# A hybrid block on one core: the reciprocal of two softmax sums made by GpSimd as a power, not by VectorE

## The reference, cut to what matters

```python
def _gated_bottleneck(x2d, conv_w, conv_b, gamma, beta, lin_w, lin_b):
    xc = einsum('ngf,gf->ng', x2d.reshape(n, g, 4), conv_w) + conv_b
    xn = (xc - mean) * rsqrt(var + eps) * gamma + beta     # over all rows
    return gelu(xn) @ lin_w.T + lin_b                      # 256 logits a row

score_out = softmax(_gated_bottleneck(x, so_...))          # 256 scores a row
s_v, s_i = top_k(score_out, 32)
out_branch = zeros.at[s_i].add(take(x @ weight, s_i) * s_v)
score_in = softmax(_gated_bottleneck(x, si_...))
s_v, s_i = top_k(score_in, 32)
in_branch = zeros.at[s_i].add(take(x, s_i) * s_v) @ weight
return out_branch + in_branch + bias
```

## Time and profile before

| what | value |
| --- | --- |
| runs | 1357.16, 1364.52 and 1355.29 us, median 1357.16 us |
| the profiled execution | 1359.22 us, of which the span of the trace is 1357.5 us |
| mean granted clock of TensorE | 0.974 of full speed |
| busy share of the span | PE 90%, DVE 85%, ACT 78%, POOL 70% |
| sparse layer 1 (tile 0 to tile 31 on GpSimd) | 271.8 to 488.8 us |
| sparse layer 2 | 1170.2 us to the end |

### The profile page before, as it was taken

One profiled execution on the slowest core, in us unless ns is written; L12 is line 12 of the kernel. 1 busy time (PEld: TensorE's weight loads), 2 busy tenths in 40 slices (PEclk: granted clock), 3 DMA queues, 4 the chain that ended last, 5 costly groups with the idle time before them and its releaser, 6 DMA issues.

```text
span 1357.5 us, 30767 instructions
## 1 busy us (share of the span) xinstructions
PE 1222.2 (90%) x10252; PEld 751.2 (55%) x10252; DVE 1147.6 (85%) x3124; ACT 1052.3 (78%) x2347; POOL 954.4 (70%) x1098
## 2 busy tenths in 40 slices
PE   5999999688888889999999999999999999677776
PEld 2555554345445546666666666666666666344443
DVE  7999996797999988888777788877878854899998
ACT  3323424786999889999999989999999985877776
POOL 4367553486787777777776777777777773488887
PEclk9999999996999999999999999999999999898988
DMA  6200000100002000010000000000000000000000
GB/s 153 61 1 1 0 0 1 42 1 1 24 28 77 30 20 24 24 25 25 25 25 2 2 2 2 2 2 3 2 2 2 2 2 1 1 31 17 32 17 31
DMA packets 35529, 25.32 MB, mean 19 GB/s; under 512 B 16358, under 2 KB 32044, under 8 KB 35372
## 3 DMA queue, kind: packets, MB, share of 16 engines
q1 hardware_dynamic: 35372, 23.36, 6.1%
HBM read 14.89 MB, written 8.39 MB: 17 GB/s over the span
## 4 chain that ended last, share of the span: by engine, by line
PE 45%; ACT 12%; issue 11%; DVE 9%; POOL 4%; DVEq 0%; DMA 0%; ACTq 0%; POOLq 0%; SPq 0%
PE banks L2123 7%; PE banks L2125 7%; PE banks L2111 6%; PE banks L2064 4%; PE banks L2140 4%; PE banks L2141 4%; DVE arena L1595 4%; PE banks L2142 4%; ACT arena L1218 3%; DVE arena L1590 3%; ACT arena L1230 2%; PE banks L2040 2%; ACT arena L1066 2%; PE banks L2186 1%; PE banks L1987 1%
## 5 line engine op out<-in xcount | busy, mean ns | idle before, releaser
L877 POOL TENSOR_TENSOR arena<-arena 128x512 f16<-128x512 f32 x383 | 437.5, 1161 | 145.1 <-ACT arena L1230 141.3
L1218 ACT ACTIVATE arena<-banks 128x512 f32<-128x512 f32 x512 | 302.6, 599 | 41.8 <-PE banks L2125 37.4
L1674 DVE TENSOR_REDUCE arena<-banks 128x1 f32<-128x512 f32 x512 | 326.3, 680 | 4.8 <-PE banks L2111 2.6
L1230 ACT ACTIVATE arena<-arena 128x512 f16<-128x512 f32 x512 | 315.6, 631 | 0.0
L2140 PE MATMUL banks<-arena 128*128 128x65 f16 x2016 | 211.4, 193 | 1.0
L2141 PE MATMUL banks<-arena 128*128 128x64 f16 x2016 | 211.6, 195 | 0.0
L2142 PE MATMUL banks<-arena 128*128 128x65 f16 x2016 | 210.6, 193 | 0.0
L1700 DVE TENSOR_TENSOR arena<-arena 128x512 f16<-128x512 f32 x129 | 107.5, 834 | 121.4 <-ACT arena L1230 121.2
L1590 DVE MAX8 arena<-arena 128x8 f32<-128x256 f32 x512 | 190.0, 412 | 23.8 <-issue 13.7
L1595 DVE MATCH_REPLACE8 arena<-arena 128x256 f32<-128x256 f32 x512 | 205.7, 409 | 0.9 <-issue 0.4
L2140 PEld LDWEIGHTS banks<-arena 128*128 128x128 f16 x2016 | 187.9, 96 | 31.7 <-issue 9.9
(11 more groups left out here) (241 smaller groups left out, 2591.7 us busy)
## 6 DMA issues: line engine op xcount, KB each, us to landing
arena<-q_store SPq DMA_DIRECT2D x48, 128.0 KB, 2.7
x<-in_L_attn_a_x SPq DMA_DIRECT2D x8, 512.0 KB, 3.9
q_store<-arena SPq DMA_DIRECT2D x32, 128.0 KB, 1.8
out<-x SPq DMA_DIRECT2D x7, 512.0 KB, 2.9
arena<-arena SPq DMA_DIRECT2D x64, 1.0 KB, 1.9
arena<-in_L_attn_a_W_in SPq DMA_DIRECT2D x1, 768.0 KB, 5.8
arena<-in_L_attn_a_W_mid SPq DMA_DIRECT2D x1, 512.0 KB, 7.4
arena<-in_L_attn_a_w_w SPq DMA_DIRECT2D x2, 256.0 KB, 7.7
```

The lines of the kernel that those rows point to most:

```text
L877: nc.gpsimd.tensor_tensor(pr_lo[c][:, kt, :], pr[:, kt, :], pr_hi[c][:, kt, :], ALU.subtract).then_inc(a_lP, 1)
L1218: nc.scalar.activation(pr[:, kt, :], ps[6 + kt % 2][:, :], ACT.Exp, scale=SM_SCALE).then_inc(a_P, 1)
L1230: nc.scalar.activation(pr_hi[c][:, kt, :], pr[:, kt, :], ACT.Copy).then_inc(a_hi, 1)
L1674: nc.vector.tensor_reduce(mx_half[c][:, i // 2, i % 2:i % 2 + 1], ps[bank][:, :], X, ALU.max).then_inc(a_mx, 1)
```

## The change

`over_sums` moves from VectorE to GpSimd. There it is the first thing of `tail`, `tail_shared` and (after the row plus bias) `tail_last`, and it makes `sm` to the power of `minus_one`, with a `tensor_tensor` of 128 x 2. VectorE's waits for `ffn_gs` and `ffn_fs` two tiles back go with it, since GpSimd's `tail` has waited for both already. VectorE gets one new wait for `f_ri`, in the last tile of layer 2.

```diff
+            def over_sums(T, p):
+                pool.wait_ge(f_e, T * 2 + 2)
+                nc.gpsimd.tensor_tensor(rinv[p], sm[p], minus_one[:, 0:2], ALU.pow).then_inc(f_ri, 1)
+
             def tail(f, t, p):
                 T = t + f * NT
-                pool.wait_ge(f_e, T * 2 + 2)
+                over_sums(T, p)
                 pool.wait_ge(f_er, T * 2 + 1 + CREDIT["f_er"])
...
             def tail_shared(t, p):
                 T = t
-                pool.wait_ge(f_e, T * 2 + 2)
+                over_sums(T, p)
                 pool.wait_ge(f_er, T * 2 + 2 + CREDIT["f_er"])
...
                 nc.gpsimd.tensor_tensor(xb[p].unsqueeze(1), x[:, t:t + 1, :], fbias[:, :].unsqueeze(1),
                                         ALU.add).then_inc(f_xb, 1)
-                pool.wait_ge(f_e, T * 2 + 2)
+                over_sums(T, p)
                 pool.wait_ge(f_er, T * 2 + 2 + CREDIT["f_er"])
...
-            def over_sums(f, t, p):
-                T = t + f * NT
-                if not (isinstance(T, int) and T < 2):
-                    dve.wait_ge(f_gs, T - 1 + CREDIT["f_gs"])
-                    dve.wait_ge(f_fs, T - 1 + CREDIT["f_fs"])
-                dve.wait_ge(f_e, T * 2 + 2)
-                nc.vector.reciprocal(rinv[p], sm[p]).then_inc(f_ri, 1)
...
                 for t in range(NT):
                     topk_first(f, t, t % 2)
-                    if t:
-                        over_sums(f, t - 1, (t - 1) % 2)
                     if f == 0:
                         head_maxima(t - 2)
                     topk_rest(f, t, t % 2)
                     if f == 0:
                         head(t)
-                over_sums(f, NT - 1, 1)
...
                 dve.wait_ge(f_gps, T + 1)
                 dve.wait_ge(f_obx, T + 1)
+                dve.wait_ge(f_ri, T + 1)
```

## The result

The kernel after takes 1376.80 us (median of 4 runs, 1374.24 to 1381.35) against 1357.01 (4 runs): a ratio of 1.0152 with an interval of 1.0127 to 1.0176. It is slower, by 1.5%. The base is the three runs shown above and a fourth of 1356.87. The profiled execution took 1374.24 us, its span is 1372.5.

What follows compares the result with a forecast made beforehand. VectorE was taken to set layer 2's pace, with GpSimd 0.40 us a tile under it. Layer 1 +4.1 and layer 2 +11.0 sum to +15.1 us: 1374.3 profiled, 1372 as median against 1357.16; range 1362 to 1383.

Steps and rivals of the forecast that it cites:

- The bound changes engine in layer 2: Layer 2: GpSimd's pace becomes 6.10 us a tile, over VectorE's 5.76, so GpSimd sets the pace; head 30 +9.4 us.
- The power's price: GpSimd's tile heads: one 128 x 2 power takes 0.70 us and costs 0.65 a tile.
- GpSimd's "own pace" of 5.45 us: Layer 2, tile 2: GpSimd waits for no other engine, 5.45 us a tile, leaving 0.40 us of room under VectorE.
- Low clock: Layer 2: waits for TensorE's in-product at low clock, formerly absorbed by GpSimd's room, now count: +1.9 us.
- The rival of many more falls: Layer 2: TensorE, left idler, falls to its low clock far more often; 1379 to 1384 us, chance 12%.
- The last two tiles: End of layer 2: +9.4 us at head 30 becomes +9.1 at the end, as L799 no longer waits for ScalarE.
- Layer 1: Layer 1: +1.9 us by tile 6, +0.2 at tile 9, +1.95 in tiles 11, 15 and 19; together +4.1.
- the first rival: Layer 1, tiles 6 to 9: the slow-clock stretch goes away, head 9 at 329.1, total +7.8 us, 1365; chance 25%.
- The base: Kernel before: profiled execution 1359.22 us, median of the runs 2.06 lower at 1357.16.

Runs made afterwards that it cites:

- e4: Kernel after with the power replaced by a multiplication by -1 of the same shape, reciprocal left out: 1354.72 us beside 1354.40 for the kernel before.
- e11: Kernel after without GpSimd's bias addition `xb` in all but each layer's last tile, power still at the head: 1377.15 us beside 1355.49 for the kernel before.
- e13: Kernel after without `xb` in all but each layer's last tile, and the power moved behind `sx`: 1354.75 us beside 1354.30 for the kernel before.
- e7: Kernel before plus an unread 128 x 4 power on GpSimd at each tile's head: 1397.20 us beside 1355.04 for the kernel before.
- e8: Kernel before plus three TensorE products of zeros ahead of the wait for `sx`, in layer 2 and layer 1's first twelve tiles: 1358.31 us beside 1355.04.
- e9: Kernel after plus three TensorE products of zeros ahead of the wait for `sx`, in layer 2 and layer 1's first twelve tiles: 1371.87 us.
- e6: Kernel before plus an unread 128 x 2 power on GpSimd at each tile's head: 1377.28 us beside 1354.40 for the kernel before.
- e1: Kernel after with the power on GpSimd in layer 2 alone, layer 1 keeping VectorE's reciprocal: 1372.24 us beside 1354.40 for the kernel before.
- e2: Kernel after with the power on GpSimd in layer 1 alone, layer 2 keeping VectorE's reciprocal: 1367.34 us beside 1354.40 for the kernel before.

## Why the prediction came out, step by step

- **The bound changes engine in layer 2: right.** Head 1 to head 30: forecast 29 x 6.10 = 176.9 and 1.9 of low-clock waits, together 178.8; measured 179.34.
- **The power's price: right.** Forecast 0.70 long and 0.65 a tile, measured 0.702 and 0.67 (5.44 to 6.11). The Trainium skill, "GPSIMD Engine Reference", section "Performance versus the Vector engine", gives elementwise operations a price by their elements and has none for a power. Priced so, it would have been like any operation of two columns; the plain one in e4 (0.195 us, nothing lost) shows what would then have happened.
- **GpSimd's "own pace" of 5.45 us: right number, wrong owner.** I read in the earlier trace rows that it waits for no other engine. It does: `ob` starts when `fs` has arrived, and no wait is shown because `xb` covers all but 0.1 us of it. The 5.45 us are the round. e11 and e13 tell the two apart. The sum came out because the power was put into the round, and because work and round are near each other: in the kernel after, L793 to L797 are 0.84 us where neighbours without a wait are 0.68 apart, so work alone would need about 6.11 - 0.16 = 5.95 us, also over 5.76. By that estimate the kernel after with `xb` kept and the power behind `sx` wins 4 to 5 us in layer 2 (29 x 0.16) and stays slower than before; this was not run.
- **Low clock: small in layer 2, as forecast, and more in the runs.** The granted clock is 0.91 after, 0.92 before in the long window; in tiles 1 to 4 it fell from 1.00 to 0.92. The rival of many more falls did not come at this length; in e7, with 0.31 us more, it did. The Trainium skill, "TensorE: Matmul & The Clock Gate", section "Part 1: The HAM clock gate", has activity release the throttle; e8 and e9, where idle time is filled and the clock rises, agree.
- **The last two tiles: too small.** From head 30 to the end of the span are 12.14 us before, 13.56 after: +1.4, where my sum had -0.3 (+9.4 at head 30, +9.1 at the end). I had tile 30's `x` no longer wait for `gs`; it waits 0.77 us. And the last in-product runs at the low clock (granted 0.50), 2.08 us against 1.21 before.
- **Layer 1: the mis-sized term.** Forecast +4.1. Tiles 1 to 6 cost +3.2 and tiles 9 to 30 +3.5, where I counted 1.9 and 2.15, and tile 0 to 1 another 1.1; tiles 6 to 9 took 21.31 us instead of 28.19, with the granted clock at 0.84 instead of 0.58: the first rival's mechanism, with head 9 at 333.04 between its 329.1 and my 336.4. So the profiled pair shows only +0.7 in layer 1, from its first logits on TensorE (260.68 before, 262.20 after) to tile 30's `x`, and another 1.5 us arose before the layer, in work that the change doesn't touch.
- **The base.** The profile of before caught the long slow stretch (0.52 of the clock from 309 to 334 us). No profile of another run shows it so: the lowest clock there is 0.74 (e6), and in e1 and e4 tiles 6 to 9 take 22 us. Before has medians of 1354.3 to 1355.5 us on the chips of the experiments, so against those, though on other chips, the change costs 21 to 22 us, where I summed 15.1. Of the difference layer 1 is 2 to 5 us (over the same part of the layer 214.78 us in e1, 221.28 after, 224.37 in e2, less the 4.1 that I gave it) and the last two tiles 1.7; the rest is not accounted for. A base some 2 us too high and a cost 6 to 7 too small leave the median 4.8 us above my number.
- **Luck.** The profiled execution took 1374.24 us, where I summed 1374.3. That is no proof of the sum: of the 15.0 us that the span grew, 1.5 arose before layer 1 (forecast: nothing), 0.7 in layer 1 (4.1) and the other 12.8 behind it (11.0). The errors cancel, since the long slow stretch in this profile of before went away.

## What to carry to other kernels

An engine that shows no wait between two heads can still be paced by a round through other engines, when some filler of its own covers the wait. Before adding work to it, follow one result out and back (here `sx`, `sT`, `fs`, `ob`) and ask whether the new instruction stands in that round or in its filler. In the kernel without `xb` the same 0.7 us cost 22 us at the head of the tile and nothing two places later.

## What was not expected of the hardware

- A GpSimd power costs by columns even when tiny: 0.551, 0.702 and 1.013 us for 128 x 1, 2 and 4, the same for ones as for sums, where a multiplication of 128 x 2 takes 0.195 us. VectorE's reciprocal of the same two columns cost 0.07 us in the queue, and freeing it was worth nothing.
- Holding TensorE's clock up with products of zeros (0.91 to 0.98 from 1170 us on) did not pay for itself: 1.0014 [0.9998, 1.0031].
